# A graph layer's first edge pass: four buffers of exponentials, node work one group later, gathers released by the sum of five groups back

## The reference

```python
# layer 0: softmax over the incoming edges, feature by feature
m = relu(x[src]) + 1e-7
ex = exp(m - seg_max[dst])
msg = seg(ex / seg(ex)[dst] * m)
x = layernorm(x + (x + msg) @ W0 + b0)
# layer 1: eight heads of 12
q, k, v = x @ Wq + bq, x @ Wk + bk, x @ Wv + bv
e = edge_attr @ We + be
s = exp(clip((k[src] * q[dst] / sqrt(12) * e).sum over a head, -5, 5))
x = layernorm(x + seg(v[src] * s) / (seg(s) + 1e-6))
```

## Time and profile before

| | us |
|---|---|
| time, median of 3 runs | 4892.83 (4892.27 to 4892.83) |
| span of the profiled execution | 4892.4 |
| PE busy | 3098.1 (63%) |
| POOL busy | 3143.9 (64%) |
| DVE busy | 2300.2 (47%) |
| ACT busy | 870.5 (18%) |

### The profile page before, as it was taken

How to read it: one execution, slowest core, us unless ns; L and a number is a source line. 1 busy time by engine, 2 the same in 40 slices (tenths; PEclk the granted TensorE clock), 3 DMA queues, 4 the chain that set the end, 5 groups by cost and what they waited for, 6 DMA issues and landing times.

```text
span 4892.4 us, 43885 instructions
## 1 busy us (share of the span) xinstructions
PE 3098.1 (63%) x13152; PEld 2767.9 (57%) x13152; DVE 2300.2 (47%) x5605; ACT 870.5 (18%) x1966; POOL 3143.9 (64%) x3330
## 2 busy tenths in 40 slices
PE   3445444555555455455578777878777877877777
PEld 3344434444444444444477677767677777767676
DVE  5434344334433443344445555555555555555555
ACT  1222222222222222222201111111111111111111
POOL 6666666666666666666566666666666666666665
PEclk8666666666656667656665655565666565566665
DMA  3111111121111111111244444444444444444443
GB/s 97 40 40 43 42 39 40 40 45 40 40 44 41 39 40 45 40 39 40 67 111 111 114 112 114 112 111 117 112 111 111 114 112 114 112 114 110 115 113 98
DMA packets 290371, 383.51 MB, mean 78 GB/s; under 512 B 154382, under 2 KB 196911, under 8 KB 290127
## 3 DMA queue, kind: packets, MB, share of 16 engines
q0 software_dynamic: 132864, 251.83, 21.4%
q1 hardware_dynamic: 157263, 128.81, 9.5%
HBM read 360.62 MB, written 19.72 MB: 78 GB/s over the span
## 4 chain that ended last, share of the span: by engine, by line
POOL 31%; issue 23%; PE 18%; another core or an unknown queue 15%; DVE 9%; DMA 2%; ACT 2%; DVEq 0%; SPq 0%; ACTq 0%
POOL rows L454 31%; PE banks L605 4%; PE banks L586 4%; PE banks L577 4%; PE banks L547 3%; DVE onehot L817 2%; PE banks L596 2%; DMA rows<-in_x,src_i 1%; DVE sums L942 1%; DVE ex L930 1%; DMA rows<-key_value,src_i 1%; DVE banks L850 1%; ACT onehot_t L717 1%; DVE sums L940 1%
## 5 line engine op out<-in xcount | busy, mean ns | idle before, releaser
L454 POOL DMA_INDIRECT rows<-key_value,src_i x1661 | 1571.9, 946 | 922.2 <-issue 431.8
L454 POOL DMA_INDIRECT rows<-in_x,src_i x1661 | 1570.6, 946 | 811.6 <-issue 469.1
L547 PE MATMUL banks<-ex,onehot 128*128 128x192 f32 x3322 | 1036.0, 483 | 1026.7 <-DVE ex L930 810.5
L547 PEld LDWEIGHTS banks<-ex,onehot 128*128 128x128 f32 x3322 | 865.2, 288 | 1188.8 <-DVE ex L930 933.9
L586 PE MATMUL banks<-qw,onehot_t 128*128 128x192 f32 x1664 | 609.2, 515 | 401.2 <-ACT onehot_t L717 233.1
L605 PEld LDWEIGHTS banks<-onehot,vals 128*104 128x104 f32 x3322 | 601.2, 272 | 260.2 <-issue 210.3
L605 PE MATMUL banks<-onehot,vals 128*104 128x64 f32 x3322 | 608.2, 359 | 183.8 <-issue 151.5
L586 PEld LDWEIGHTS banks<-qw,onehot_t 128*128 128x128 f32 x1664 | 440.3, 302 | 449.1 <-ACT onehot_t L717 258.4
L577 PE MATMUL banks<-we_sb,ea 97*128 97x96 f32 x3322 | 672.1, 372 | 0.0
L577 PEld LDWEIGHTS banks<-we_sb,ea 97*128 97x128 f32 x3322 | 662.2, 295 | 0.0
L930 DVE SCALAR_TENSOR_TENSOR ex<-banks,ex 128x384 f32<-128x384 f32 x416 | 229.0, 550 | 795.7 <-issue 654.5
(11 more groups left out here) (107 smaller groups left out, 1480.4 us busy)
## 6 DMA issues: line engine op xcount, KB each, us to landing
ea<-in_edge_t SPq DMA_DIRECT2D x415, 192.0 KB
rows<-in_x,src_i POOLq DMA_INDIRECT x1661
rows<-key_value,src_i POOLq DMA_INDIRECT x1661
qw<-query SPq DMA_DIRECT2D x832, 24.0 KB
key_value<-qkv SPq DMA_DIRECT2D x24, 400.0 KB
x<-in_x SPq DMA_DIRECT2D x7, 672.0 KB, 8.2
query<-qkv SPq DMA_DIRECT2D x24, 192.0 KB
out<-outs SPq DMA_DIRECT2D x24, 192.0 KB
```

The source lines that it names most:

```text
L454: pool.indirect_dma_start(out=to[0:n, r, u, :], out_offset=None, in_=table, in_offset=bass.IndirectOffsetOnAxis(ap=src_i[0:n, g * G + u:g ...
L547: last = nc.tensor.matmul(ps_sum0[b], onehot[:, r, u, :], ex[:, b, u, :], start=u == 0, stop=u == n - 1)
```

## The change

- `ex` gets four buffers (`RX`) instead of two, and every reader and writer takes `g % RX`.
- `relu_rows` waits for the product of group g-2 instead of its sum. `exp_rows` waits for the sum of group g-4, whose buffer it writes over.
- DVE's loop is written anew: at step g it adds group g-2 (`BACK` = 2), makes the comparison for g+1, then the product of g, then the node stages of g-2.
- `node_stages` on PE is called with g-2 instead of g-1, on ACT with g-3 instead of g-2.
- POOL waits ahead of group g for the sum of group g-5 (`PACE0`) instead of g-3. The start, 2(g-8), stays, and so does the second layer's `PACE`.

```diff
@@ buffers and constants
+RX = 4
+BACK = 2
+PACE0 = 5
...
-        ex = sb("ex", [P, 2, G, 2 * D])
+        ex = sb("ex", [P, RX, G, 2 * D])
@@ POOL
-                    pool.wait_ge(s_sum, min(g - PACE, 2 * (g - R0)) + 1)
+                    pool.wait_ge(s_sum, min(g - PACE0, 2 * (g - R0)) + 1)
@@ PE
                 for g in range(NG):
                     sum_rows(g)
-                    node_stages(g - 1)
-                for at in range(NG - 1, NG + 9):
+                    node_stages(g - BACK)
+                for at in range(NG - BACK, NG + 9):
                     node_stages(at)
@@ ACT
                     if g >= 2:
-                        act.wait_ge(s_sum, g - 1)
+                        act.wait_ge(s_p, g - 1)
...
                 def exp_rows(g):
                     b, n = g % 2, tiles_of_group(g)
                     act.wait_ge(s_relu, g + 1)
-                    nc.scalar.activation(ex[:, b, 0:n, 0:D], ps_relu[b][:, 0:n, :], ACT.Exp,
+                    if g >= RX:
+                        act.wait_ge(s_sum, g - RX + 1)
+                    nc.scalar.activation(ex[:, g % RX, 0:n, 0:D], ps_relu[b][:, 0:n, :], ACT.Exp,
...
-                    node_stages(g - 2)
-                for at in range(NG - 2, NG + 9):
+                    node_stages(g - BACK - 1)
+                for at in range(NG - BACK - 1, NG + 9):
@@ DVE
                 make_onehot0(0)
-                make_onehot0(1)
-                for g in range(NG + 1):
+                for g in range(NG + BACK):
+                    h = g - BACK
+                    if h >= 0:
...
+                        add_rows(h, ats[k], ats[k + 1])
+                    if g + 1 < NG:
+                        make_onehot0(g + 1)
                     if g < NG:
                         weigh_rows(g)
                     if g == R0:
                         scale_weights()
-                    if g:
...
-                        add_rows(g - 1, ats[k], ats[k + 1])
-                    if g + 2 < NG:
-                        make_onehot0(g + 2)
-                    if g:
-                        node_stages(g - 1)
+                    if h >= 0:
+                        node_stages(h)
```

More of the change, by code:

```diff
@@ L546, in sum_rows @@
                     for u in range(n):
-                        last = nc.tensor.matmul(ps_sum0[b], onehot[:, r, u, :], ex[:, b, u, :],
+                        last = nc.tensor.matmul(ps_sum0[b], onehot[:, r, u, :], ex[:, g % RX, u, :],
                                                 start=u == 0, stop=u == n - 1)
@@ L929, in weigh_rows @@
                     dve.wait_ge(s_exp, g + 1)
-                    V.scalar_tensor_tensor(out=ex[:, b, 0:n, D:2 * D], in0=ps_relu[b][:, 0:n, :], scalar=EPS_MSG,
-                                           in1=ex[:, b, 0:n, 0:D], op0=ALU.add, op1=ALU.mult).then_inc(s_p, 1)
+                    V.scalar_tensor_tensor(out=ex[:, g % RX, 0:n, D:2 * D], in0=ps_relu[b][:, 0:n, :], scalar=EPS_MSG,
+                                           in1=ex[:, g % RX, 0:n, 0:D], op0=ALU.add, op1=ALU.mult).then_inc(s_p, 1)
                 def add_rows(g, low, high):
@@ L965, in _ @@
                 make_onehot0(0)
-                make_onehot0(1)
-                for g in range(NG + 1):
+                for g in range(NG + BACK):
+                    h = g - BACK
+                    if h >= 0:
+                        if h % 2 == 0:
+                            m = min(2, NG - h)
+                            ats = nc.values_load_multi_w_load_instructions(
+                                halves[0:1, h:h + m, :].rearrange("p a b -> p (a b)"),
+                                engines=[DVE_ENGINE], min_val=0, max_val=(SLOTS - 1) * W0,
+                                skip_runtime_bounds_check_because=why)[1]
+                        k = 2 * (h % 2)
+                        add_rows(h, ats[k], ats[k + 1])
+                    if g + 1 < NG:
+                        make_onehot0(g + 1)
                     if g < NG:
@@ L971, in _ @@
                         scale_weights()
-                    if g:
-                        if (g - 1) % 2 == 0:
-                            m = 2 * min(2, NG - g + 1)
-                            ats = nc.values_load_multi_w_load_instructions(
-                                halves[0:1, g - 1:g - 1 + m // 2, :].rearrange("p a b -> p (a b)"),
-                                engines=[DVE_ENGINE], min_val=0, max_val=(SLOTS - 1) * W0,
-                                skip_runtime_bounds_check_because=why)[1]
-                        k = 2 * ((g - 1) % 2)
-                        add_rows(g - 1, ats[k], ats[k + 1])
-                    if g + 2 < NG:
-                        make_onehot0(g + 2)
-                    if g:
-                        node_stages(g - 1)
+                    if h >= 0:
+                        node_stages(h)
                 for at in range(NG, NG + 7):
```

## The result

| | before | after |
|---|---|---|
| time, median of 13 runs each | 4892.23 (4889.77 to 4895.22) | 4905.18 (4900.94 to 4909.53) |
| span of the profiled execution | 4892.4 | 4906.7 |

The ratio is 1.0026, 95% interval [1.0019, 1.0033]: slower by 0.26%, where 4603 us were forecast. None of the gain is there.

A forecast was written before the change was run, and what follows sets the result against it. Layer one was taken as bound by POOL's gathers plus its waits for late sums. 4892.8 - 293.1 (waits removed) + 3 (clusters falling on chunk work) = 4602.7, so 4603 us; range 4583 to 4650.

The forecast's parts named there:

- What bounds the kernel: First layer: POOL's gathers at 1.251 us, 5.00 us a group, plus its waits for late sums, making 5.74 us a group.
- the gain of POOL's lead: First layer: two more groups of lead, 10.0 us, outlast every late sum; worth 293.1 us, the whole gain.
- every wait of steady state goes: POOL's first-layer waits for sums vanish, the longest being 4.8 us; excess 299.9 us, of which 6.8 at the start stays.
- What is late next: Check that product, sum and addition recover between late sums: 58.6 against 85 us per chunk; 3 us left for collisions.
- the 2.77 us a group: Pace of product, sum and addition when not short of rows, from 24.9/9 at the start of layer one.
- tied to POOL: Rival: POOL's issuing holds PE's signals, so a longer lead only lengthens each hold; time stays 4893, chance 0.07.
- DVE's order: DVE's loop keeps its cycle; only node work moves behind the next product; worth 0, ends of -10 and +10 us.
- Node stages one group later: PE and ACT node stages come one group later; cost 0, up to one group's 5 us once at the end.
- The slower rival: PE's projection waits for ACT's copies behind one more group's exp; 120 us at most, half taken: 4953, chance 0.04.
- PE's busy time should not change: Sign to check: PE's busy time must not change by more than the clock makes it.
- The sentence of the Trainium skill: Profiler estimates matmul ends; PE might really work until 1008.2 and be the bound at 5.74 us a group, time staying 4893.

The follow-up runs named there:

- e9: Kernel before with one number changed: first-layer POOL waits for the sum five groups back, not three; 4192.3 us beside 4192.4, prompt condition.
- e12: Kernel before with SP loading straight rows in layer one, plus 1000 POOL gathers that nobody reads; 4968.7 us beside 4900.5, late condition.
- e11: Kernel before with SP loading straight rows of x in layer one, POOL issuing nothing there; 3707.3 us beside 4857.8, late condition.
- e8: Kernel before with SP loading straight rows of x in layer one, POOL issuing nothing there; 3339.7 us beside 4192.4, prompt condition.
- e18: Kernel before with SP loading straight rows in layer one, plus 1000 POOL fills that nobody reads; 3775.5 us beside 4888.3, late condition.

## Why the prediction was wrong, point by point

**What bounds the kernel: half right.** POOL's own 1.25 us a gather, and waits for late sums on top, 5.74 us a group: so it was, and the prompt condition shows the 5.00 us bare (e9).

**The failed step is the gain of POOL's lead, "every wait of steady state goes".** It took a late sum for something of a fixed length (4.8 us of POOL's waiting at the most) which 10.0 us of lead outlast. The term of the sum is -293.1 us, and it measured as nothing: the excess of POOL's waits is 342.0 - 133 x 0.308 = 301.0 us against 299.9. What the runs show in its place is that PE's completions creep while POOL gathers (e12: 24 us a group), and that most of them come out in POOL's pauses (83 of 97, 97 of 129). POOL stops until an older sum is out, the sums fall two groups further behind, and each pause still lets out what it did: as many pauses, as far apart as before. The account for the single pause is argued from these counts; the lead alone never met the late condition.

**What is late next: the 2.77 us a group were measured in the wrong place.** The earlier trace rows lie at the start of the layer, where eight groups are ready and POOL soon waits. In those 25 us of the kernel before POOL stopped at 63.14 and twice more:

```profile
74.07 0.94 POOL L454 DMA_INDIRECT rows<-in_x,src_i  x1 [1.24 <-PE banks L547]
...
80.62 0.94 POOL L454 DMA_INDIRECT rows<-in_x,src_i  x1 [1.86 <-PE banks L547]
```

Three pauses released signals there. The catch-up rate was one of a POOL that stops every 6 to 11 us, used for a POOL that would never stop, where e12 measured 24 us a group. It was not wrong for every stretch of unbroken gathers: in the kernel after, PE ran 24 rows, three groups, from 1006.12 to 1013.01, in the first 10 us after a pause.

**The counter-evidence was misread.** The rival "tied to POOL" stood in the prediction with its mechanism word for word, and got 0.07, since one signal came after only 1.07 us of stop. But that row too lies in a stop of POOL: its row before had ended at 999.34, and the signal was there at 1000.5. Both late signals of the earlier trace rows came while POOL stood. A row that fits both theories was counted against one, and the count that bears on it, 83 of 97 in a pause, was not made. That rival forecast 4893.

**DVE's order at 0, ends -10 and +10: right within its ends, in the prompt condition.** There order alone cost 3 us (1.0007, 1.0008), in the finishing of the last nodes; in the late condition it was not seen alone. **Node stages one group later, 0 to 5 us once at the end: right in place, short in size** for the whole change: the pause between the layers grew by 12.4 us, where order alone added 2 to 4. Which part of the remaining 8 us is the lead's backlog, and which the late condition's, stays open: lead alone never met the late condition.

**The slower rival** (120 us at the most through ACT's copies) did not happen. ACT's waits ahead of x1t did grow (72.6 to 216.8 us), beside a pace that POOL's stops set.

**PE's busy time should not change; it fell** from 1184.3 to 1029.4 us in the stage, at 0.66 and 0.67 of the clock. A sum's matmul takes 439 ns by the page now, 483 before. Ends of matmuls are modelled, so I draw nothing from it.

**The sentence of the Trainium skill** ("Perfetto Trace Analysis", Tensor Engine Instruction: ends are estimated) gave 4893, near the result, and the prediction set it aside on the strength of the earlier trace rows, from the start of the layer. The runs do not refute it in full. That PE's work is the bound whatever POOL does is refuted (e11: 1199 us for the layer with the same sums). But in e12, where one matmul row is done every 2.80 us, PE may well be working on a sum long after the modelled end of its rows. That no run settles.

## What to carry to other kernels

Before you give a waiting engine more lead, ask what the late thing was waiting for: look at whether the releases fall into the waiter's own pauses. If they do, as here, a longer lead can lengthen the lateness and buy nothing. What would help (fewer gathers issued, or pauses that release more groups) was not tried on a kernel that computes the reference. And take a catch-up rate only from a stretch in which the other engines do what they will do in the changed kernel.

## What the runs showed of the hardware

- The same program on these chips runs in two conditions some 16% apart: 4192 to 4203 us and 4855 to 4901 us. In the slower one PE's completions come late in the first layer with POOL's gathers, and not without them (e8 and e11: 1199 us in both for a layer without gathers).
- There, 1000 gathers on which nothing depends slow a stream of PE, ACT and DVE from 2.9 to 24 us a group (e12); 1000 fills on the same engine, 1.06 us each, leave it at 2.95 (e18). The lateness outlasts the last gather by some 25 us (1413.74 to 1440.3).
- During that run of gathers one matmul row of PE was done every 2.80 us, whatever matmul it was: 22.43 us for a sum's eight rows, 11.16 us for the four of the transposes.
- Neither lead, nor order, nor less work of PE moved the prompt condition by over 0.1%: there the first layer is POOL's 1.25 us a gather and nothing else.
